# Four-layer graph network: last layer begun with four pairs of row tiles, its negations on ScalarE

## The reference

```python
mask = adj > 0
head = mask / max(sqrt(sum(mask*mask, -1)), EPS)
inc  = adj + head
edge_fea = inc @ cur                      # cur = relu(layernorm(x)), 4096 x 256
return edge_fea / sum(inc, -1)
```

## Time and profile before

| | us |
|---|---|
| median of three runs | 1314.26 |
| lowest, highest | 1310.81, 1326.79 |
| the profiled execution: its time, its span | 1318.66, 1316.9 |
| mean granted TensorE clock | 0.996 |
| busy: PE, DVE, ACT, POOL | 1265.0, 1006.4, 631.3, 362.4 |

### The profile page before, as it was taken

The page is one execution under the profiler, slowest core; times in us unless marked ns, Lnnn a source line. Parts: engine busy times, 40 slices in busy tenths (PEclk is TensorE's granted clock), DMA queues, the critical chain, the costliest instruction groups (busy, mean ns, idle before and its releaser), DMA issues.

```text
span 1316.9 us, 26797 instructions
## 1 busy us (share of the span) xinstructions
PE 1265.0 (96%) x9548; PEld 944.1 (72%) x9548; DVE 1006.4 (76%) x2273; ACT 631.3 (48%) x1480; POOL 362.4 (28%) x422
## 2 busy tenths in 40 slices
PE   6999999979999999989999999999999988799998
PEld 4788888854555555557777777777777766688887
DVE  7979888899355555579989978988889997776542
ACT  6665545456222232266556766756666654211111
POOL 2000000012322223213233223232333332466433
PEclk9999999999999999999999999999999998999999
DMA  9999999922121120125753553644544423351500
GB/s 245 265 331 336 332 373 386 369 80 85 48 65 57 57 65 17 49 89 160 201 175 107 181 172 105 189 149 143 175 145 149 137 89 95 81 149 33 143 26 25
DMA packets 122899, 199.95 MB, mean 152 GB/s; under 512 B 13200, under 2 KB 83856, under 8 KB 122768
## 3 DMA queue, kind: packets, MB, share of 16 engines
q1 hardware_dynamic: 115568, 194.04, 47.0%
q10 hardware_dynamic: 7200, 4.20, 1.1%
HBM read 147.85 MB, written 50.33 MB: 150 GB/s over the span
## 4 chain that ended last, share of the span: by engine, by line
PE 63%; DVE 13%; issue 6%; DMA 5%; POOL 3%; ACT 2%; SPq 1%; ACTq 0%; DVEq 0%; POOLq 0%
PE ps L1770 11%; PE ps L1865 10%; PE ps L1657 8%; PE ps L1658 8%; PE ps L1755 7%; PE ps L1756 7%; DMA acc<-in_adj 5%; DVE ring L828 4%; PE ps L1787 4%; PE ps L1826 3%; DVE small L840 2%; POOL ring L726 1%; SPq L464 1%; DVE ring L1076 1%; ACT hs L1524 1%
## 5 line engine op out<-in xcount | busy, mean ns | idle before, releaser
L726 POOL TENSOR_TENSOR ring<-ring 128x512 f16<-128x512 f32 (+2 forms) x133 | 149.3, 1123 | 358.3 <-ACT ring L1531 358.3
L1619 PE MATMUL ps<-val_hi,ring 128*128 128x257 f16 x1024 | 225.2, 273 | 0.0
L1620 PE MATMUL ps<-val_lo,ring 128*128 128x256 f16 x1024 | 225.2, 273 | 0.0
L1657 PE MATMUL ps<-ring,acc 128*128 128x512 fp8e4 x512 | 195.1, 381 | 8.4 <-DVE acc L966 8.4
L1770 PE MATMUL ps<-hnt 128*128 128x512 f16 (+3 forms) x864 | 196.3, 363 | 0.6 <-DVE ring L1076 0.4
L1658 PE MATMUL ps<-ring,acc 128*128 128x512 fp8e4 x512 | 194.9, 381 | 0.0
L828 DVE STREAM_TRANSPOSE ring<-acc 128x1024 uint8<-128x1024 uint8 x128 | 151.0, 1220 | 29.1 <-DMA acc<-in_adj 28.9
L1410 ACT ACTIVATE hnt<-ring 128x512 bf16<-128x512 uint8 (+1 forms) x192 | 115.2, 604 | 75.8 <-DVE ring L828 75.8
L1755 PE MATMUL ps<-val_hi,hs 128*128 128x257 f16 x534 | 146.2, 274 | 1.6 <-DVE acc L1139 1.4
L1787 PE MATMUL ps<-val_hi,hs 128*128 128x257 f16 x534 | 146.2, 274 | 0.0
L1756 PE MATMUL ps<-val_lo,hs 128*128 128x256 f16 x534 | 146.0, 273 | 0.0
(11 more groups left out here) (234 smaller groups left out, 2393.8 us busy)
## 6 DMA issues: line engine op xcount, KB each, us to landing
acc<-in_adj SPq DMA_DIRECT2D x256, 256.0 KB, 8.6
turned_dram<-ring SPq DMA_DIRECT2D x56, 512.0 KB, 2.9
ring<-turned_dram SPq DMA_DIRECT2D x224, 128.0 KB, 2.9
at_dram<-ring SPq DMA_DIRECT2D x32, 512.0 KB, 9.2
ring<-at_dram SPq DMA_DIRECT2D x64, 256.0 KB, 4.0
ring<-at_dram SPq DMA_DIRECT2D x24, 512.0 KB, 3.9
ring<-at_dram SPq DMA_DIRECT2D x9, 1024.0 KB, 9.7
xs<-in_x SPq DMA_DIRECT2D x12, 256.0 KB, 9.6
```

The source lines that it names most:

```text
L726: nc.gpsimd.tensor_tensor(lo2[m % 2][:, k:GW], p2t[m % 2][:, k:GW], hi2[m % 2][:, k:GW], ALU.subtract).then_inc(sem["lo2_done"], 1)
L1619: nc.tensor.matmul(ps[:, k % 8, 0:D + 1], lhs, val_hi0[:, t, 0:D + 1], start=(t == 0), stop=False)
L1620: last = nc.tensor.matmul(ps[:, k % 8, 0:D], lhs, val_lo0[:, t, :], start=False, stop=(t == NB - 1))
L1657: nc.tensor.matmul(ps[:, bank + c, :], g_hi[:, t, c * P:(c + 1) * P], src, start=(t == 0), stop=False)
```

## The change

- **Four pairs begin.** Pair 0 now uses PSUM banks 2 and 3, which also hold the later three products of every pair. So PE starts pairs 1, 2, 0, 3, takes products 0 to 2 of all four for k below 12, then d2, then k = 12 to 15, and must then wait until ACT has copied pair 0's four products out (`copied` at 4) before d1 of pair 0.
- **d2 in quarters, d7 later.** The first set's d2 is made in four pieces between the tail items of groups 6 and 7. Its d7, in four pieces in steps 111 to 114 before, is now made after d6, just ahead of the first `two_tiles`.
- **Tail of group 5.** `CLOSE` moves items 13 to 16 one step later, item 16 two; `CLOSE_ACT` moves items 13 and 15 one later.
- **Negation on ACT.** For sets 1 to 3 DVE's `edge_mask` and `sign` go. ACT computes `-v + 2**-100` into fp8 in place, a quarter of the tile (128 x 2048 bytes) an instruction.
- **ACT's order.** For pairs 0 to 2 ACT copies the next pair's four products right after a pair's fifth copy, then negates (four quarters, three, one), and then issues the stores.
- **Set 1's differences** are made in the order d5, d2, d1, d6, d7, the order of their use; d2 behind `two_tiles(2)`, the last three ahead of `two_tiles(4)`.

```diff
-        CLOSE = {... 12: 5, 13: 6, 14: 7, 15: 7, 16: 8}
-        CLOSE_ACT = {10: 4, 12: 6, 13: 6, 15: 8}
+        CLOSE = {... 12: 5, 13: 7, 14: 8, 15: 8, 16: 10}
+        CLOSE_ACT = {10: 4, 12: 6, 13: 7, 15: 9}
-            PREP[opens[5] + 7 + r] = ("d7", "a12", r)
# DVE, before the last layer
             dve.wait_ge(sem["lo2_done"], NM)
-            dif2(0)
-            group_tail(NG - 1, 10)
-            for i in range(13, TAIL):
-                group_tail(NG - 2, i)
+            dif2(0, 0)
+            dif2(0, 1)
+            group_tail(NG - 2, 15)
+            dif2(0, 2)
+            group_tail(NG - 2, 16)
+            dif2(0, 3)
             for i in range(11, TAIL):
                 group_tail(NG - 1, i)
             dif1(0)
             dif6(0)
+            for r in range(4):
+                dif7(0, r)
# DVE, the loop over pairs
+                if n == GB:
+                    dif1(1)
+                    dif6(1)
                 if p > 0 and i == 0:
                     dif7(p)
-                    if not last:
-                        edge_mask(p + 1, "a11")
+                elif n == 2:
+                    dif5(1)
+                elif n == 3:
+                    dif2(1)
+                elif i == 2 and not last:
                     dif5(p + 1)
                     dif1(p + 1)
                 elif i == 3 and not last:
                     dif2(p + 1)
-                    if p > 0:
-                        dif6(p + 1)
+                    dif6(p + 1)
# ACT
+            def negate(p, k, quarters):
+                act.wait_ge(raw_loaded[k[1:]], 16 * (p + 1))
+                act.wait_ge(sem["half_set"], 3)
+                for r in quarters:
+                    v = homes[kept[p][k]][:, r // 2, 4 * (r % 2):4 * (r % 2) + 4, :]
+                    last = nc.scalar.activation(v, v, ACT.Identity, bias=speck, scale=-1.0, saturate=False)
+                    if r == 3:
+                        last.then_inc(sem["negated"], 1)
+            copy_four(0)
             for n in range(NB // 2):
                 act.wait_ge(sem["products_done"], products(n, 1))
                 nc.scalar.activation(copies[4], halves_of(n, 4), ACT.Copy)...
+                if n < 3:
+                    copy_four(n + 1)
+                if n == 0:
+                    negate(1, "a11", range(4))
+                elif n == 1:
+                    negate(1, "a22", range(3))
+                elif n == 2:
+                    negate(1, "a22", range(3, 4))
                 for half, k in enumerate(reversed(rows_of(n))):
                     ... store_out(act, ...)
+                if 3 <= n < NB // 2 - 1:
+                    copy_four(n + 1)
+                if n % GB < 2 and GB <= n < NB // 2 - GB:
+                    negate(n // GB + 1, ("a11", "a22")[n % GB], range(4))
# PE
-            for n in range(3):
+            for n in (1, 2, 0, 3):
...
+            pe.wait_ge(sem["copied"], 4)
```

More of the change, by code:

```diff
@@ L39 @@
 group_out rden_ready rsc_ready x3_done stats3_done var3_ready rstd3_ready nm3_ready h3_done hi3_done lo3_done
-plain_low sums_made sums_high edge_mask negated dif5_done difs_done dif7_done
+plain_low sums_made sums_high edge_mask negated dif5_done dif2_part difs_done dif7_done
 three_done products_done copied side_done tiles_step epi_done3 out_stored_a out_stored_b""".split()
@@ L173, in gnn_kernel @@
         one = col(GB)
+        speck = col(1)
         bn = [col(6) for _ in range(2)]
@@ L379, in gnn_kernel @@
         WIDE_ACT = {10: 7, 12: 9, 13: 10, 15: 12}
[L380 to L381 removed]
+        CLOSE = {0: 0, 1: 0, 2: 0, 3: 1, 4: 1, 5: 1, 6: 2, 7: 2, 8: 2, 9: 2, 10: 3, 11: 5, 12: 5, 13: 7, 14: 8, 15: 8, 16: 10}
+        CLOSE_ACT = {10: 4, 12: 6, 13: 7, 15: 9}
         FINAL = {0: 0, 1: 0, 2: 0, 3: 1, 4: 1, 5: 2, 6: 2, 7: 3, 8: 3}
@@ L419, in product @@
         def product(n, j):
-            bank = (4 + 2 * (n % 3) + j // 2) % 8 if j < 4 else 2 if j == 4 or (j == 6 and n == LAST) else 3
+            bank = (4 + 2 * ((n - 1) % 3) + j // 2) % 8 if j < 4 and n > 0 else 2 + j // 2 if j < 4 else 2 if j == 4 or (j == 6 and n == LAST) else 3
             half = j % 2 if j < 4 else j // 6
@@ L430, in products, with differences @@
         def products(n, j):
-            return 4 * n + j + 1 if n > 2 else n + 1 if j == 0 else 3 + 3 * n + j
+            return 4 * n + j + 1 if n > 3 else n + 1 if j == 0 else 4 + 3 * n + j
+        def differences(p, step):
+            return step - 1 if p == 0 else 3 * p - 1 + step
         def rows_of(n):
@@ L604, in _ @@
                     load_raw(sp, n // GB + 2, "12")
-                    sp.wait_ge(sem["difs_done"], 3 * (n // GB + 1) + 2)
+                    sp.wait_ge(sem["difs_done"], differences(n // GB + 1, 2))
                     load_raw(sp, n // GB + 2, "21")
@@ L620, in _ @@
             pool.memset(one, 1.0).then_inc(sem["half_set"], 1)
-            pool.wait_ge(sem["half_set"], 2)
+            pool.memset(speck, 2.0 ** -100).then_inc(sem["half_set"], 1)
+            pool.wait_ge(sem["half_set"], 3)
             nc.gpsimd.tensor_tensor(f3[:, 0:GB], one, half[:, 0:GB], ALU.pow).then_inc(sem["power_set"], 1)
@@ L1220, in sign @@
                 v = words(kept[p][k], r)
-                step = 4 * (k == "a22") + r + 1 if r is not None else 8 + 2 * (p - 1) + (k == "a22") + 1
-                dve.wait_ge(sem["edge_mask"], step)
+                dve.wait_ge(sem["edge_mask"], 4 * (k == "a22") + r + 1)
                 nc.vector.tensor_scalar(v, v, NEG_EDGES, None, ALU.bitwise_and).then_inc(sem["negated"], 1)
@@ L1240, in dif1, with dif2 @@
                                                ALU.bitwise_and, ALU.bitwise_xor).then_inc(sem["difs_done"], 1)
-            def dif2(p):
+            def dif2(p, r=None):
                 if p > 0:
@@ L1247, in dif2 @@
                 dve.wait_ge(sem["negated"], negated(p, "a22"))
-                nc.vector.tensor_tensor(words(kept[p]["d2"]), words(kept[p]["a21"]), words(kept[p]["a22"]),
-                                        ALU.bitwise_xor).then_inc(sem["difs_done"], 1)
+                nc.vector.tensor_tensor(words(kept[p]["d2"], r), words(kept[p]["a21"], r), words(kept[p]["a22"], r),
+                                        ALU.bitwise_xor).then_inc(sem["difs_done" if p > 0 else "dif2_part"], 1)
             def dif6(p):
-                dve.wait_ge(sem["difs_done"], 3 * p + 2)
+                if p == 0:
+                    dve.wait_ge(sem["dif2_part"], 4)
+                else:
+                    dve.wait_ge(sem["difs_done"], differences(p, 2))
                 dve.wait_ge(sem["negated"], negated(p, "a11"))
@@ L1271, in prepare @@
                     sign(0, k, r)
-                elif what == "d5":
+                else:
                     dif5(0, r)
-                else:
-                    dif7(0, r)
             def two_tiles(n):
@@ L1354, in _ @@
             group_tail(NG - 1, 9)
+            group_tail(NG - 2, 13)
+            group_tail(NG - 2, 14)
+            group_tail(NG - 1, 10)
             dve.wait_ge(sem["lo2_done"], NM)
-            dif2(0)
-            group_tail(NG - 1, 10)
-            for i in range(13, TAIL):
-                group_tail(NG - 2, i)
+            dif2(0, 0)
[4 more added lines that the diff above has]
+            dif2(0, 3)
             for i in range(11, TAIL):
@@ L1381, in _ @@
                 elif i == 3 and not last:
-                    if p == 0:
-                        dif5(1)
-                        dif1(1)
                     dif2(p + 1)
-                    if p > 0:
-                        dif6(p + 1)
[L1388 to L1396, removed]
+                    dif6(p + 1)
                 two_tiles(n)
@@ L1590, in _, with copy_four @@
                 group_tail(NG - 1, i)
-            for n in range(NB // 2):
+            def copy_four(n):
                 act.wait_ge(sem["three_done"], n + 1)
@@ L1599, in _ @@
                     nc.scalar.activation(copies[j], halves_of(n, j), ACT.Copy).then_inc(sem["copied"], 1)
+            def negate(p, k, quarters):
[7 more added lines that the diff above has]
+            copy_four(0)
+            for n in range(NB // 2):
                 act.wait_ge(sem["products_done"], products(n, 1))
@@ L1878, in last_three @@
                 since(pe, sem["copied"], 5 * n)
-                pe.wait_ge(sem["difs_done"], 3 * p + 2)
+                pe.wait_ge(sem["difs_done"], differences(p, 2))
                 for k in range(NB // 2):
@@ L1883, in last_three @@
                 since(pe, sem["tiles_step"], 4 * (n - 1) + 2)
-                pe.wait_ge(sem["difs_done"], 3 * p + 3)
+                pe.wait_ge(sem["difs_done"], differences(p, 3))
                 for k in range(NB // 2):
@@ L1897, in _ @@
             pe.wait_ge(sem["acc_added"], n_outer[NS])
-            for n in range(3):
-                first_three(n)
-                if n == 2:
+            first_three(0)
+            for n in (1, 2, 0, 3):
+                if n == 0:
```

(17 more changed lines are left out.)

## The result

| | us |
|---|---|
| changed kernel, median of 12 runs (lowest, highest) | 1310.39 (1303.4, 1325.39) |
| kernel before, median of 12 runs beside them | 1317.31 (1309.22, 1326.97) |
| ratio, 95% interval | 0.994 (0.9912 to 0.9968) |

The change takes 4 to 12 us off. The profiled execution of the changed kernel has a span of 1322.5 us, longer than that of before, because it fell in a disturbed run: 11.8 us of it are lost in the DMA-bound layers before 570 us, so stretches are compared from a mark that both traces have, PE's wait of 3.1 us in the attention's last part (1071.26 before, 1082.95 after).

A forecast was written before the change was run, and what follows sets the result against it. DVE's fixed order was taken to bound the attention's end, PE the last layer apart from 8.6 us of waits. Terms -3.0 and -0.6 ahead of the last layer and +2.0 in it gave -1.6, hence 1312.7 us, range 1305 to 1320.

The forecast's parts named there:

- The tail of group 5: Attention's end: items moved later let PE resume 3.0 us earlier, bounds -1.6 and -4.4.
- the clock stays up: Rival, attention's end: the shorter PE wait keeps the clock at 2.4 GHz, about 2.2 us gained, 1310.5 us; chance 0.15.
- The first set's d7: Attention steps 111 to 114: removing d7 brings -0.6 us, between 0 and -1.8; free behind d6.
- Four pairs: Last layer's start: three waits vanish, 3.4 us; a new wait of 0.15 for pair 0's banks.
- ScalarE's negations: Last layer on ACT: 1.97 us a quarter; PE waits 3.5 us before pair 2 and 4.1 before pair 3.
- Behind them on ACT stand four stores: Step within the negations: stores take 1.9 us of ACT after the quarters, ahead of the next pair's fifth copy.
- The slower rival: Rival, last layer: new waits bring the clock down, two falls cost 5.3 us, 1318.0 us; chance 0.28.
- The second set: Last layer, pair 4: PE loses 0.1 and 1.0 us waiting for DVE's differences, where it lost 0.62 + 0.15.
- Sets 2 and 3: Last layer: PE waits 0.7 us at pair 7 and at pair 11, between 0 and 1.2.
- ScalarE isn't late: Rival, last layer: quarters of 1.1 us or stores issued during computing remove both ACT waits, 1305.1 us; chance 0.10.

The follow-up runs named there:

- e1: Kernel before with only the changed kernel's tables CLOSE and CLOSE_ACT; ratio to the kernel before 0.9964 (0.9921 to 1.0006).
- e3: Changed kernel with the tables CLOSE and CLOSE_ACT of the kernel before; ratio to the kernel before 0.9958 (0.9919 to 0.9998).
- e2: Kernel before with only the first set's d7 moved behind d6; one run, last layer 206.96 us against 204.51 before.
- e5: Changed kernel with ScalarE's four stores of each pair issued by SyncE; one run, last layer 201.42 us against 203.28.
- e6: Changed kernel with the stores of pairs 0 to 2 ahead of the negations; one run, last layer 217.65 us against 203.28.

## Why the prediction was right, and where it was wrong

**The time and the sign** came out right, the size did not: -1.6 us forecast, -4 to -12 measured, -6.3 in the traces. Of the 4.7 us between, 2.2 are the clock, which the forecast left as it was, and 3.2 the last layer, which it made 2.0 us longer and which became 1.2 us shorter; the tail and d7 together gave 0.7 less than forecast. That 1312.7 lies so near the measured 1310.39 is partly luck: it starts from a median of three runs, 1314.26, where twelve gave 1317.31, and from that the same 1.6 would have given 1315.7.

**The tail of group 5.** Forecast -3.0 to PE's restart, measured -2.73, by the steps given: the exponentials free step 140 (its weights stand 1.64 us earlier against the mark, 1.6 forecast), `next_rows` holds step 141. e1 and e3 bear it out alone.

**The clock.** I gave "the clock stays up" 0.15 and 1310.5 us. It stayed up in the changed kernel's trace and brought 2.17, as priced (2.2). The text took from the wait of 3.10 at the mark, where it had stayed up in one trace, that such a wait does not bring the clock down; in six of the fourteen traces it did. The runs show that both happen at the new length of wait too, with 1.2 to 1.5 us lost when it falls for 3.4 us, never the 6.8 us of before. So even the bad case gains 0.7 to 1.0 us (2.2 less 1.2 to 1.5); my forecast, which kept the whole loss, had no case for that.

**The first set's d7.** Forecast -0.6 and free at its new place. Ahead of the mark the two traces differ by 0.14. The cover was real: without it 2.4 us, as e2 shows and the text said.

**Four pairs.** Forecast -3.4 and 0.15 for pair 0's banks; the three waits went, and PE's timeline shows no wait there.

**ScalarE's negations: the step that failed.** A quarter took 1.89 us from start to start (7.68 for all four; 1.97 a quarter forecast). But the step "Behind them on ACT stand four stores (1.79, with the gap 1.9)" counted these as time of ACT ahead of the fifth copy. They are issued while the negations compute (e5: without them the same waits to 0.01). Forecast 3.5 and 4.1, measured 0.75 and 1.36 with 0.15 each. Of the 2.6 us less in the first, 1.9 are the stores, 0.3 the quarters and the rest rounding and an earlier copy. In the second the stores fall out once more (1.9), and the copies and three quarters took 0.6 less than forecast. The slower rival, which lived on waits above 3.1 in the last layer, fell with them. (Its price has a slip: two falls at the middle of 1.7 to 3.4 are 5.1, not 5.3.) That falls there cost much, e6 shows, behind waits of 6.66 and 5.49.

**The second set.** Forecast 1.1, measured 0.38 + 0.82 + 0.73 and 0.15 each, 2.4. PE came to pair 4 at 52.0 in place of 57.0 after the layer's start, DVE's chain ended only 3.8 earlier. Its d1, d6 and d7 took 2.29, 2.70 and 2.81, the last two beside POOL operations of 2.77, as forecast. Sets 2 and 3 cost 1.5 where I had 1.4, but at pairs 8, 11 and 12.

**In sum** the last layer went from 8.7 us over the 195.8 without waits to 7.5, not to 10.5. The rival "ScalarE isn't late" named "stores that issue while it computes" as one of its causes, and that is what happened; its price was too high, since 2.1 us of waits for ACT are left (2.4 with their 0.15 each).

## What to carry to other kernels

When long instructions are put ahead of DMA issues on the same engine, the issues cost nothing here, as what they wait for was done before the last of these instructions ended; put the other way round, the wait stands bare and everything behind it is late. Ask of a moved piece of work which idle stretch of its engine it fits (a11's 7.7 us fitted 7.6 us of nothing) before asking what it costs where it stands. And in a stretch bound by one engine's order, what counts is the one instruction that the next engine waits for: pieces in front of it are worth their full length, until the wait behind it becomes the bound.

## What the runs showed of the hardware that was not expected

- ACT's queue issued four DMAs in the middle of a run of four ACTIVATEs that precede them in the program, 1.7 us before the last of these began (1150.61 and 1152.28).
- A wait of PE of 3.4 us brought its clock from 2.4 to 1.2 GHz in some executions and not in others, with the same program around it; 4.3 to 4.4 us did in all four traces, and for twice as long (6.8 us against 3.4). A wait of 3.1 us did so in six traces of fourteen, once for 6.8 us. Two shorter waits close together (1.50 and 1.98) did so once, in e1_tail.
- Negation in fp8 on ACT with a pointer bias took 1.99 to 2.10 us for 2,048 elements; the Trainium skill's page "ScalarE: Activation LUTs", section "What ACT_TABLE_LOAD costs", gives about 1.99 us for that size in fp32 and bf16. No table load shows in front of the first.
